# Pairing products and outputs on TensorE, and the chain's residue before the last corner's sum

## Chip, cores and metric

The kernel runs on one core of a Trainium2 chip. The metric is the device time of one execution in microseconds; the time before is the median of three runs.

## What is computed

x is 2 x 1024 x 256 in float32. A first layer adds a product with one 256 x 256 matrix per batch element, chosen by a category id. The second layer is a mixture of one chosen MLP and two shared ones, with a gate made from the first token:

```python
x = x + einsum('bsd,bdh->bsh', x, W[cat_ids]) + b[cat_ids][:, None, :]
s0, s1 = relu(x @ swi[0]) @ swo[0], relu(x @ swi[1]) @ swo[1]
eo = relu(x @ wi[type]) @ wo[type]                      # D=256, F=1024
w = softmax(relu(concat(eo[:, 0], s0[:, 0], s1[:, 0]) @ g1) @ g2)
x = x + eo * w[:, 0] + s0 * w[:, 1] + s1 * w[:, 2]
```

## The kernel before

Every float32 matrix is split into a rounded part (hi) and a residue (lo), both fp32r, and every product is a triple of matmuls: hi by hi, hi by lo, lo by hi (`three`, line 750). A tile is 128 partitions by 512 tokens.

The MLPs run as six passes over pairs of 512-token tiles, four groups of 256 hidden features each: groups j = 0 to 23. Groups 0 and 1 are computed directly. Groups 2 to 23 use seven products instead of eight for the 2 x 2 block product (hidden features by input features by two token tiles). TensorE runs product 1, then adds products 6, 7 and 4 into the same PSUM bank, `chain`; after each of the first three ScalarE copies the bank's running value into `kept` (line 396). Product 2 goes to the bank `left`, product 5 to `right`, product 3 is added to `right`. VectorE (line 534) adds kept 0 to left, makes `corner` = right + kept 2 between products 5 and 3, and adds kept 1 to right after product 3. The four hidden tiles are thus left (i = 0), chain (1), corner (2), right (3). For each ScalarE writes h_hi = relu (line 408) and VectorE the residue h_lo (line 529), in the order 0, 2, 1, 3. Product 1 of the next group may start once h_lo of chain is made, product 5 once h_lo of right is made, product 3 once corner is made, and products 6, 7 and 4 once kept 0, 1 and 2 are copied.

The outputs of group j, u = 0 to 7, are triples too: hidden tile u // 2 times one of two weight blocks, added up over four groups in the banks acc. They are run inside group j + 1, among its products, in an order written out by hand. In short, p for products of group j and o for outputs of group j - 1: p1 p2 o0 p6 p5 o1 p7 o2 o3 p4 p3 o4 o5 o6 o7.

Each engine runs its instructions in program order. Special groups carry more work behind or between the hidden tiles:

- Group 2: ScalarE casts three parts of x (line 389), VectorE makes their residues (line 516). Group 3: ScalarE casts four tiles of input sums (line 415), one before h_hi of corner, one between h_hi of corner and of chain, two at the end. Groups 5, 6, 9, 10: two such casts at the end.
- Groups 4, 8, 12, 16: ScalarE copies acc of a finished pass into y (line 487) behind h_hi of right; output 0 and 1 of the next group wait for it. Groups 5, 9, 13, 17: VectorE does the same for the other side (line 693), then gate partial sums (lines 550, 553).
- Group 18: VectorE reduces the gate (line 567) behind h_lo of right, ScalarE gathers the result with four copies (line 502), VectorE goes on. Group 19: softmax (lines 596 to 604, exponentials on ScalarE, line 506) and additions of whole tiles to x (line 612). Group 20: additions from acc (line 623), one behind h_lo of corner and one behind h_lo of chain, then more tiles.

GpSimd makes the sums of weight blocks (lines 290, 304), the weight residues m_lo and the residues of the input sums; weights come by DMA two groups ahead.

Of the kernel before, what the change touches and what calls it, by code (L numbers as in the profile page):

```python
# [46 lines left out]
def build(nc, x_t, cat_w, cat_b, mlp_w, ids, g1, g2, out_t):  # L47
# [7 lines left out]
    with ExitStack() as ctx:  # L55
# [150 lines left out]
        def nth(j, i):  # L206
            return i + 1 if j < DIRECT else NTH[i]
# [10 lines left out]
        def before(j, each):  # L218
            return (j - DIRECT) * each
# [294 lines left out]
        def _(dve):  # L514
# [12 lines left out]
            def hidden_lo(j, i):  # L527
                dve.wait_ge(h_hi_ready, 4 * j + nth(j, i))
                nc.vector.scalar_tensor_tensor(out=h_lo[:, j % 2, i, :], in0=hidden[i][:], scalar=0.0,  # L529
                                               in1=h_hi[:, j % 2, i, :].bitcast(F32), op0=ALU.max, op1=ALU.subtract  # L530
                                               ).then_inc(h_split, 1)
# [83 lines left out]
            def add_acc(q, side, d):  # L615
                kind, pair = PASSES[q]
                b, t = PAIRS[pair][side]
                dve.wait_ge(outputs_done, acc_done(q, side, d))
                if kind == 1:
                    dve.wait_ge(added[b][t], 1)  # L620
                else:
                    dve.wait_ge(added[b][t], 2 + d)
                nc.vector.scalar_tensor_tensor(out=x1_part(b, t, d), in0=acc[side][d][:], scalar=mix[:, b, kind:kind + 1],
                                               in1=x1_part(b, t, d), op0=ALU.mult, op1=ALU.add
                                               ).then_inc(last_added if kind == 2 else added[b][t], 1)
# [56 lines left out]
            for j in range(DIRECT, N):  # L682
                q = (j - 1) // GROUPS - 1
                dve.wait_ge(left_done, before(j, 1) + 1)
                dve.wait_ge(kept_ready, before(j, 3) + 1)
                add_kept(left, left, 0)
                if j == KEPT * GROUPS + 3:
                    gate_spread()
                if j % GROUPS == 1 and q >= 0:
                    for d in range(DC):  # L690
                        if q < KEPT:
                            dve.wait_ge(outputs_done, acc_done(q, 1, d))
                            nc.vector.tensor_copy(y_part(q, 1, d), acc[1][d][:]).then_inc(y_second, 1)
                        else:
                            add_acc(q, 1, d)
                hidden_lo(j, 0)
                if j == KEPT * GROUPS + 2:
                    gate_transpose()
                dve.wait_ge(right_done, before(j, 2) + 1)
                dve.wait_ge(kept_ready, before(j, 3) + 3)  # L700
                add_kept(corner, right, 2)
                hidden_lo(j, 2)
                if j == KEPT * GROUPS + GROUPS:
                    add_acc(KEPT, 0, 0)
                dve.wait_ge(right_done, before(j, 2) + 2)
                add_kept(right, right, 1)
                hidden_lo(j, 1)
                if j == KEPT * GROUPS + GROUPS:
                    add_acc(KEPT, 0, 1)
                hidden_lo(j, 3)  # L710
                if j == 2:
                    for n in range(3, 6):
                        part_lo_of(n)
                if j % GROUPS == 1 and 0 <= q < KEPT:
                    gate_partial(q)
                if j == KEPT * GROUPS + 2:
                    gate_quarters()
                    gate_logits()
                if j == KEPT * GROUPS + 3:
                    gate_max()  # L720
                    gate_softmax()
                    add_tile(0, 1)
                    add_tile(1, 0)
                if j == KEPT * GROUPS + 4:
                    add_tile(0, 0)
                    add_tile(1, 1)
                if j == KEPT * GROUPS + 5:
                    add_tile(2, 0)
                    add_tile(2, 1)
                if j == KEPT * GROUPS + 6:  # L730
                    add_tile(3, 0)
                    add_tile(3, 1)
# [13 lines left out]
        def _(pe):  # L746
# [116 lines left out]
            def product(j, n):  # L863
                q = j // GROUPS
                pair = PASSES[q][1]
                alpha, beta = PAIRS[pair]
                new_pair = j % GROUPS == 0 or j == DIRECT
                slot = j % SLOTS
                if n == 1:
                    pe.wait_ge(m_split, first_part(j))  # L870

                    pe.wait_ge(h_split, 4 * (j - 1) + nth(j - 1, 1))
                    if new_pair:
                        pe.wait_ge(part_split, 1 + max(part_no(alpha, 0), part_no(alpha, 1), part_no(beta, 1)))
                    three(chain, m_hi, A11, slot, *part(part_no(alpha, 0)), True, True).then_inc(chain_done, 1)
                if n == 2:
                    three(left, m_hi, A12, slot, *part(part_no(alpha, 1)), True, True).then_inc(left_done, 1)
                if n == 6:
                    if new_pair:
                        pe.wait_ge(t_split, 4 * pair + 2)  # L880
                    pe.wait_ge(m_split, second_part(j))
                    pe.wait_ge(kept_ready, before(j, 3) + 1)
                    three(chain, m_hi, S2, slot, *t_sum(pair, 1), False, True).then_inc(chain_done, 1)
                if n == 5:

                    pe.wait_ge(h_split, 4 * (j - 1) + nth(j - 1, 3))
                    three(right, m_hi, S1, slot, *t_sum(pair, 0), True, True).then_inc(right_done, 1)
                if n == 7:
                    if new_pair:
                        pe.wait_ge(t_split, 4 * pair + 3)  # L890
                    pe.wait_ge(kept_ready, before(j, 3) + 2)
                    three(chain, m_hi, S3, slot, *t_sum(pair, 2), False, True).then_inc(chain_done, 1)
                if n == 4:
                    if new_pair:
                        pe.wait_ge(t_split, 4 * pair + 4)
                    pe.wait_ge(kept_ready, before(j, 3) + 3)
                    three(chain, m_hi, A22, slot, *t_sum(pair, 3), False, True).then_inc(chain_done, 1)
                if n == 3:

                    pe.wait_ge(hidden_ready, before(j, 3) + 2)  # L900
                    three(right, m_hi, S4, slot, *part(part_no(beta, 1)), False, True).then_inc(right_done, 1)

            def output(j, u):
                i, d = u // DC, u % DC
                side, f = i // 2, (0, 1, 1, 0)[i]
                q = j // GROUPS
                first, final = j % GROUPS == 0 and i in (0, 2), j % GROUPS == GROUPS - 1 and i in (1, 3)
                if d == 0:
                    pe.wait_ge(h_split, 4 * j + nth(j, i))
                if u == 0 and j < DIRECT:  # L910
                    pe.wait_ge(m_split, second_part(j))
                if first:

                    if q == 0:
                        pe.wait_ge(x1_ready, 4 + side * DC + d + 1)
                    elif q <= KEPT:
                        pe.wait_ge((y_first, y_second)[side], (q - 1) * DC + d + 1)
                    else:
                        b, t = PAIRS[PASSES[q][1]][side]
                        pe.wait_ge(added[b][t], 2 + d)  # L920
                last = three(acc[side][d], m_hi, WO + f * D + d * P, j % SLOTS,
                             h_hi[:, j % 2, i, :], h_lo[:, j % 2, i, :], first, final)
                last.then_inc(outputs_done, 1)
# [20 lines left out]
            for u in range(8):  # L944
                output(0, u)
            for j in range(DIRECT, N):
                product(j, 1)
                product(j, 2)
                output(j - 1, 0)
                product(j, 6)  # L950
                product(j, 5)
                output(j - 1, 1)
                product(j, 7)
                output(j - 1, 2)
                output(j - 1, 3)
                product(j, 4)
                product(j, 3)
                for u in range(4, 8):
                    output(j - 1, u)
            for u in range(4):  # L960
                output(N - 1, u)
            for d, columns in ((0, slice(0, TOK)), (1, slice(0, TOK // 2)), (1, slice(TOK // 2, TOK))):
# [45 lines left out]
```

## Time and profile before

| | us |
|---|---|
| median of 3 runs | 268.51 (268.29 to 270.18) |
| the profiled execution | 268.48 |
| its span on the core | 266.6 |
| TensorE busy | 262.1 |
| VectorE, ScalarE, GpSimd busy | 163.4, 149.9, 162.2 |

Start times in the trace count from the span's start. A matmul's duration is modelled and overlaps the next one, so TensorE's pace is read from the distance of its starts. An engine's instruction may likewise start before the recorded end of the one ahead.

### The profile page before, as it was taken

The page shows a single profiled execution, that of the slowest core. Times are in us where ns is not written, and L with a number is a line of the kernel's source. Part 1 is how long each engine was busy: PE and PEld are TensorE (multiplying, and loading weights), DVE is VectorE, ACT ScalarE, POOL GpSimd, SP SyncE. Part 2 cuts the span into 40 slices and gives each one's busy share as a digit, 9 for nine tenths or more (in the row PEclk, how much of TensorE's full clock was granted, in tenths as well). Part 3 has the DMA queues.
Part 4 walks back from the last instruction along what each step waited for, and adds up shares of the span by engine and source line. Part 5 has one row for each costly group of instructions (what it writes and reads, how often), then busy time and mean ns, then how long its engine had stood idle before and what let it go on. Part 6 is the DMA issues. An engine that isn't in the chain of part 4 may idle for free.

```text
span 266.6 us, 3455 instructions
## 1 busy us (share of the span) xinstructions
PE 262.1 (98%) x1158; PEld 217.1 (81%) x1158; DVE 163.4 (61%) x246; ACT 149.9 (56%) x267; POOL 162.2 (61%) x171
## 2 busy tenths in 40 slices
PE   7999999999999999999999999999999999999995
PEld 7788888888888888888888888888888888888884
DVE  3779968635645435654445565345476577985664
ACT  3596457766576555665655744646545755645320
POOL 0269999999958949838944725625626528535000
DMA  5744322012022012102022012022022022000404
GB/s 167 216 168 157 121 79 80 14 69 80 1 81 79 18 61 79 68 16 79 0 79 81 26 53 81 9 71 80 2 79 79 0 79 76 6 0 0 157 4 157
DMA packets 7473, 18.31 MB, mean 69 GB/s; under 512 B 1312, under 2 KB 2080, under 8 KB 7456
## 3 DMA queue, kind: packets, MB, share of 16 engines
q1 hardware_dynamic: 6736, 16.92, 19.2%
q10 hardware_dynamic: 720, 1.18, 1.4%
q8 instruction: 9, 0.15, 0.2%
q14 instruction: 8, 0.07, 0.1%
HBM read 16.00 MB, written 2.10 MB: 68 GB/s over the span
## 4 chain that ended last, share of the span: by engine, by line
PE 97%; DMA 1%; DVE 1%; issue 0%; DVEq 0%
PE acc L750 48%; PE chain L750 23%; PE right L750 12%; PE left L750 6%; PE acc L759 4%; DMA x<-x_t 1%; PE left L805 1%; PE chain L805 1%; PE corner L750 1%; PE corner L805 1%; PE right L805 1%; DVE x_hi L640 0%; DVE x_lo L516 0%; DVE x L741 0%; DVEq L740 0%
## 5 line engine op out<-in xcount | busy, mean ns | idle before, releaser
L290 POOL TENSOR_TENSOR m_lo<-staged,m_hi 128x512 fp32r<-128x512 f32 (+2 forms) x49 | 82.9, 1704 | 76.5 <-ACT m_hi L372 62.5
L750 PE MATMUL acc<-h_lo,m_hi 128*128 128x512 f32 x190 | 73.9, 389 | 0.0
L750 PE MATMUL acc<-h_hi,m_lo 128*128 128x512 f32 x190 | 73.9, 389 | 0.0
L750 PE MATMUL acc<-h_hi,m_hi 128*128 128x512 f32 x190 | 73.9, 389 | 0.0
L396 ACT COPY kept<-chain 128x512 f32<-128x512 f32 x66 | 38.8, 587 | 52.7 <-PE chain L750 52.7
L750 PEld LDWEIGHTS acc<-h_hi,m_hi 128*128 128x128 f32 x190 | 35.7, 188 | 7.5
L750 PEld LDWEIGHTS acc<-h_lo,m_hi 128*128 128x128 f32 x190 | 35.7, 188 | 7.4
L750 PEld LDWEIGHTS acc<-h_hi,m_lo 128*128 128x128 f32 x190 | 35.7, 188 | 7.4
L529 DVE SCALAR_TENSOR_TENSOR h_lo<-left,h_hi 128x512 fp32r<-128x512 f32 x24 | 16.6, 691 | 28.2 <-ACT h_hi L408 28.2
L290 POOL TENSOR_TENSOR staged<-staged 128x128 f32<-128x128 f32 x66 | 31.0, 485 | 1.7
L534 DVE TENSOR_TENSOR left<-left,kept 128x512 f32<-128x512 f32 x22 | 15.3, 695 | 23.3 <-PE left L750 23.3
L529 DVE SCALAR_TENSOR_TENSOR h_lo<-corner,h_hi 128x512 fp32r<-128x512 f32 x24 | 16.6, 690 | 16.3 <-ACT h_hi L408 16.3
L534 DVE TENSOR_TENSOR corner<-right,kept 128x512 f32<-128x512 f32 x22 | 15.4, 698 | 18.2 <-ACT kept L396 18.2
L750 PE MATMUL chain<-t_hi,m_lo 128*128 128x512 f32 x66 | 25.7, 389 | 0.0
L750 PE MATMUL chain<-t_hi,m_hi 128*128 128x512 f32 x66 | 25.7, 389 | 0.0
L750 PE MATMUL chain<-t_lo,m_hi 128*128 128x512 f32 x66 | 25.7, 389 | 0.0
L408 ACT ACTIVATE h_hi<-right 128x512 fp32r<-128x512 f32 x24 | 14.4, 599 | 18.7 <-DVE right L534 18.3
L408 ACT ACTIVATE h_hi<-corner 128x512 fp32r<-128x512 f32 x24 | 14.4, 601 | 18.4 <-DVE corner L534 18.3
L372 ACT CAST m_hi<-staged 128x896 fp32r<-128x896 f32 x22 | 20.8, 944 | 0.0
L529 DVE SCALAR_TENSOR_TENSOR h_lo<-right,h_hi 128x512 fp32r<-128x512 f32 x24 | 16.6, 690 | 3.1 <-ACT h_hi L408 0.3
L290 POOL TENSOR_TENSOR t_lo<-t_raw,t_hi 128x512 fp32r<-128x512 f32 x12 | 15.3, 1294 | 2.5 <-ACT t_hi L415 2.5
L529 DVE SCALAR_TENSOR_TENSOR h_lo<-chain,h_hi 128x512 fp32r<-128x512 f32 x24 | 16.3, 680 | 0.3 <-ACT h_hi L408 0.3
(151 smaller groups left out, 439.8 us busy)
## 6 DMA issues: line engine op xcount, KB each, us to landing
staged<-mlp_w SPq DMA_DIRECT2D x22, 512.0 KB, 3.3
x<-x_t ACTq DMA_DIRECT2D x4, 256.0 KB, 3.6
staged<-mlp_w SPq DMA_DIRECT2D x4, 256.0 KB, 3.2
x<-x_t SPq DMA_DIRECT2D x4, 256.0 KB, 5.0
out_t<-x SPq DMA_DIRECT2D x2, 512.0 KB, 4.8
g_sb<-g SPq DMA_DIRECT2D x1, 768.0 KB, 3.8
out_t<-x SPq DMA_DIRECT2D x3, 256.0 KB, 2.3
w_raw<-cat_w SPq DMA_DIRECT2D x4, 128.0 KB, 2.4
```

Source lines behind the costliest of these rows:

```text
L290: return nc.gpsimd.tensor_tensor(out, a, b, ALU.subtract)
L372: nc.scalar.copy(m_hi[:, j % SLOTS, 0:PLAIN], staged[:, j % 2, 0:PLAIN]).then_inc(m_hi_ready, 1)
L396: nc.scalar.copy(kept[:, n, :], chain[:]).then_inc(kept_ready, 1)
L408: nc.scalar.activation(h_hi[:, j % 2, i, :], hidden[i][:], ACT.Relu).then_inc(h_hi_ready, 1)
L529: nc.vector.scalar_tensor_tensor(out=h_lo[:, j % 2, i, :], in0=hidden[i][:], scalar=0.0, in1=h_hi[:, j % 2, i, :].bitcast(F32), op0=ALU.ma ...
L534: nc.vector.tensor_tensor(out[:], product[:], kept[:, n, :], ALU.add).then_inc(hidden_ready, 1)
L750: last = nc.tensor.matmul(out[:, columns], half[:, slot, at:at + P], moving[:, columns], start=(start and n == 0), stop=(stop and n == 2), ...
L759: return nc.tensor.matmul(acc[t][d][:], w[:, b, at:at + P], x_part(x, b, t, i), start=start, stop=stop)
L805: return nc.tensor.matmul(hidden[i][:], w[:, 0, at:at + P], moving, start=start, stop=stop, skip_group_check=True)
```

## The change

On TensorE the order inside a group becomes p1 p2 o0 o1 p6 p5 o2 o3 p7 o4 o5 p4 p3 o6 o7: two products, two outputs, throughout, with product 7 alone. On VectorE the residue of the chain's tile, `hidden_lo(j, 1)`, stands ahead of the sum into right instead of behind it. The instructions themselves, their tiles and their semaphores are the same.

```diff
@@ -702,9 +702,9 @@
                 hidden_lo(j, 2)
                 if j == KEPT * GROUPS + GROUPS:
                     add_acc(KEPT, 0, 0)
+                hidden_lo(j, 1)
                 dve.wait_ge(right_done, before(j, 2) + 2)
                 add_kept(right, right, 1)
-                hidden_lo(j, 1)
                 if j == KEPT * GROUPS + GROUPS:
                     add_acc(KEPT, 0, 1)
                 hidden_lo(j, 3)
@@ -944,19 +944,22 @@
             for u in range(8):
                 output(0, u)
             for j in range(DIRECT, N):
+
                 product(j, 1)
                 product(j, 2)
                 output(j - 1, 0)
+                output(j - 1, 1)
                 product(j, 6)
                 product(j, 5)
-                output(j - 1, 1)
-                product(j, 7)
                 output(j - 1, 2)
                 output(j - 1, 3)
+                product(j, 7)
+                output(j - 1, 4)
+                output(j - 1, 5)
                 product(j, 4)
                 product(j, 3)
-                for u in range(4, 8):
-                    output(j - 1, u)
+                output(j - 1, 6)
+                output(j - 1, 7)
```

## Rows read from the trace of the kernel before

**Rows 1.** The page: busy us (share of the span) and instructions of each engine.
```profile
PE 262.1 (98%) x1158; PEld 217.1 (81%) x1158; DVE 163.4 (61%) x246; ACT 149.9 (56%) x267; POOL 162.2 (61%) x171
```

**Rows 2.** The page: the chain that ended last, shares by engine.
```profile
PE 97%; DMA 1%; DVE 1%; issue 0%; DVEq 0%
```

**Rows 3.** Stretches: length, busy us of five engines, clock, DMA share, GB/s; group 6.
```profile
74.50:84.70 10.20, 10.20 (x47) 8.45 (x46) 5.16 (x8) 6.43 (x11) 6.63 (x5) 1.00 0.19 65
```

**Rows 4.** Timeline of TensorE: start us, duration, what; product 1 of groups 10, 11.
```profile
115.16 0.39 PE L750 MATMUL chain<-part_hi,m_hi 128*128 128x512 f32 x1
...
125.36 0.39 PE L750 MATMUL chain<-part_hi,m_hi 128*128 128x512 f32 x1
```

**Rows 5.** Timeline of ScalarE in group 10, from the third kept copy on.
```profile
120.12 0.59 ACT L396 COPY kept<-chain 128x512 f32<-128x512 f32 x1 [0.45 <-PE chain L750]
121.60 0.60 ACT L408 ACTIVATE h_hi<-corner 128x512 fp32r<-128x512 f32 x1 [0.90 <-DVE corner L534]
122.22 0.60 ACT L408 ACTIVATE h_hi<-chain 128x512 fp32r<-128x512 f32 x1
123.63 0.60 ACT L408 ACTIVATE h_hi<-right 128x512 fp32r<-128x512 f32 x1 [0.81 <-DVE right L534]
124.12 1.13 ACT L415 CAST t_hi<-t_raw 128x512 fp32r<-128x512 f32 x2
```

**Rows 6.** Timeline of VectorE in group 10, from the sum into corner on.
```profile
120.81 0.70 DVE L534 TENSOR_TENSOR corner<-right,kept 128x512 f32<-128x512 f32 x1 [0.92 <-ACT kept L396]
122.23 0.69 DVE L529 SCALAR_TENSOR_TENSOR h_lo<-corner,h_hi 128x512 fp32r<-128x512 f32 x1 [0.72 <-ACT h_hi L408]
122.84 0.69 DVE L534 TENSOR_TENSOR right<-right,kept 128x512 f32<-128x512 f32 x1
123.45 0.68 DVE L529 SCALAR_TENSOR_TENSOR h_lo<-chain,h_hi 128x512 fp32r<-128x512 f32 x1
124.26 0.69 DVE L529 SCALAR_TENSOR_TENSOR h_lo<-right,h_hi 128x512 fp32r<-128x512 f32 x1
```

**Rows 7.** Timeline around product 3 of group 4, whose release comes late.
```profile
59.77 0.70 DVE L534 TENSOR_TENSOR corner<-right,kept 128x512 f32<-128x512 f32 x1 [1.14 <-ACT kept L396]
...
60.52 0.19 PEld L750 LDWEIGHTS right<-part_hi,m_hi 128*128 128x128 f32 x1
...
60.71 0.40 PE L750 MATMUL right<-part_hi,m_hi 128*128 128x512 f32 x1
```

**Rows 8.** Timeline of ScalarE in group 8: the two copies into y.
```profile
103.73 1.07 ACT L487 COPY y<-acc 128x512 f32<-128x512 f32 x2
```

**Rows 9.** Timelines of ScalarE and VectorE, end of group 2 to left sum of 3.
```profile
42.45 1.65 ACT L389 CAST part_hi<-x 128x512 fp32r<-128x512 f32 x3
...
43.20 3.88 DVE L516 TENSOR_TENSOR part_lo<-x,part_hi 128x512 fp32r<-128x512 f32 x3
47.00 0.69 DVE L534 TENSOR_TENSOR left<-left,kept 128x512 f32<-128x512 f32 x1
```

**Rows 10.** Timelines of VectorE and ScalarE: gate reduction, gather, first kept copy of group 19.
```profile
206.47 0.68 DVE L567 TENSOR_REDUCE gate_quarter<-gate_blocks 128x16 f32<-128x512 f32 x1
...
207.18 0.88 ACT L502 COPY gate_all<-gate_quarter 32x16 f32<-32x16 f32 x4 [1.35 <-DVE gate_quarter L567]
207.97 0.57 ACT L396 COPY kept<-chain 128x512 f32<-128x512 f32 x1
```

**Rows 11.** Timelines of ScalarE and VectorE, end of group 19 and group 20.
```profile
217.34 0.19 ACT L506 ACTIVATION_READ_ACCUMULATOR exps<-logits,neg_max 128x1 f32 x1
...
220.55 0.69 DVE L534 TENSOR_TENSOR left<-left,kept 128x512 f32<-128x512 f32 x1
...
222.34 0.59 ACT L396 COPY kept<-chain 128x512 f32<-128x512 f32 x1
...
225.06 0.74 DVE L623 SCALAR_TENSOR_TENSOR x<-acc,mix,x 128x512 f32<-128x512 f32 x1
```

**Rows 12.** Timeline of ScalarE in group 9: idle time put down to issue.
```profile
112.30 0.60 ACT L408 ACTIVATE h_hi<-chain 128x512 fp32r<-128x512 f32 x1 [0.30 <-issue]
```

## The prediction

> **What bounds the kernel now.** I read the page first. TensorE is busy for 262.1 of 266.6 us [rows 1], and the chain that ended last is TensorE for 97% [rows 2]. The stretches of one group each show it exactly: 10.20 us of TensorE in 10.20 us, at clock 1.00, while VectorE, ScalarE and GpSimd stand at 5 to 6.6 us [rows 3]. So I looked at TensorE's starts: group 10 begins at 115.16 and group 11 at 125.36 [rows 4], 10.20 us for 15 triples of matmuls, T = 0.68 us each (0.2267 per matmul). Group j begins at S(j) = 115.16 + 10.20 x (j - 10). Nothing is idle between groups 2 and 23, so a new order of the same 45 matmuls has nothing to win there; it can only lose, where a triple must now wait for ScalarE or VectorE. The question is how late their results come against the new slots.
>
> **The timetable of an ordinary group.** The order before is p1 p2 o0 p6 p5 o1 p7 o2 o3 p4 p3 o4 o5 o6 o7, after it is p1 p2 o0 o1 p6 p5 o2 o3 p7 o4 o5 p4 p3 o6 o7 (p a product of group j, o an output of group j - 1). p7 moves from slot 6 to 8, p4 from 9 to 11, p3 from 10 to 12, p6 from 3 to 4. From the group's start, before [rows 5, 6]: the third kept copy 4.96, the sum into corner 5.65, h_hi of corner 6.44, its h_lo 7.07, h_hi of chain 7.06, sum into right 7.68, h_lo of chain 8.29, h_hi of right 8.47, its h_lo 9.10. After: p7 ends at 9T = 6.12 instead of 4.76, 1.36 later, and so are the copy (6.32), the sum (7.01), h_hi of corner (7.80) and its h_lo (8.43). p4 ends at 12T = 8.16; h_hi of chain came 0.26 behind p4's end (7.06 against 6.80), so it is at 8.42 and ends 0.60 later. h_lo of chain then starts at 9.05 and lasts 0.68, to 9.73. The sum into right is now behind it: VectorE's next instruction started 0.61 after the one before (122.23, 122.84, 123.45), so it starts at 9.66; h_hi of right follows 0.79 later at 10.45, its h_lo at 11.08. **All that stands behind h_hi of right comes 1.98 us later against the groups' starts**, that is 1.36 from the slots and 0.62 from the new place of the residue.
>
> **When a late result costs.** The one place of before where a result comes at the last moment: the sum into corner ends at 59.77 + 0.70 = 60.47, the weights are loaded at 60.52, the matmul starts at 60.71, on its slot (within 0.01) [rows 7]. So a result that ends 0.19 us or more before the slot costs nothing; later, the excess is lost for good, since TensorE has no idle time to give back. In the ordinary group p1 of the next group (slot 10.20) may not overwrite chain before that h_lo ends at 9.73: wanted 10.01, margin 0.28. p3 wants the corner sum at 8.16 - 0.19 = 7.97 and has it at 7.71. p4 wants the third copy (end 6.91) at 7.29. p6 has gained a slot. So 0 there.
>
> The Trainium skill's page VectorE: DVE Perf Modes (The DRAIN you can't avoid) says that the next operation does not start until the pipe is empty, and adds that one not held starts earlier. The rows bear out only the second, 0.61 from start to start beside 0.69 to 0.70 of duration [rows 6]; by the first the residue would end 0.08 later, margin 0.20, and the sum would grow by some 0.3 in all.
>
> **The groups with extra work**, each against its slot less 0.19:
> - Group 2. Behind h_hi of right ScalarE casts three parts (1.65 for three, 0.53 apart [rows 9]). Before that cost nothing. After they start at 10.94, the first kept copy of group 3 at 12.52 and ends (0.59) at 13.10; its reader p6 has slot 10.20 + 4T = 12.92, wanted 12.73: **0.36**. VectorE's part residues and what follows took 3.80 from their start to the left sum (43.20 to 47.00 [rows 9]); they start at S(2) + 11.69 = 45.17, the left sum of group 3 at 48.97. The third copy stands 1.79 behind the left sum on ScalarE where ScalarE sets the pace (220.55, 222.34 [rows 11]): 50.76, ends 51.35; the corner sum 51.45 to 52.15. Slot of p3: 43.69 + 0.36 + 8.16 = 52.21, wanted 52.02: **0.14**. Behind it come h_hi of corner (52.24), the cast of t_hi(1,1) that the code puts there (0.50 each), and only then h_hi of chain at 53.25, h_lo from 53.88 to 54.56. p1 of group 4 wants 54.20: **0.37**. Its p6, behind two more casts, loses about **0.09**.
> - Groups 4, 8, 12, 16. ScalarE copies two accumulators into y, 1.07 for both, 0.48 apart [rows 8]. They now start at 10.94, the first ends at 11.53. It frees acc for the next group's o0, slot 11.56, wanted 11.37: **0.15** each, four times, **0.60**. Before, the first copy was done 1.8 us ahead of that slot. The term is the least certain, since the row gives only the two copies' common length: between 0 (if the first ends by 11.37) and 0.3 each. The second copy and o1 have 0.2 in hand.
> - Groups 5, 6, 9, 10 cast two tiles (1.13 [rows 5]); the kept copy then ends at 12.54, wanted 12.73: nothing, margin 0.19.
> - Gate reductions, group 18. gate_quarter stands behind h_lo of right at 206.47, the four gather copies on ScalarE start 0.71 later, and the kept copy of group 19 is queued 0.79 behind them [rows 10]. After: 11.69, 12.40, 13.19, ends 13.77, wanted 12.73: **1.04** at p6 of group 19.
> - Softmax, group 19. ScalarE's last accumulator read starts at 217.34 and takes 0.19 [rows 11], 1.47 behind the start of h_lo of right (206.96 + 9.10). After it ends at 12.54; the kept copy ends at 13.13: **0.40** at p6 of group 20. VectorE's softmax and tile additions hold the left sum until 220.55, 4.49 behind the same start: after, 5.37 into group 20, or 4.97 with the 0.40 counted; third copy 6.76 to 7.35, corner sum to 8.15, wanted 7.97 to 8.02: **0.17** over p4 and p3. Here the code also puts an accumulator's addition (0.74 long, so 0.66 to the next start by the overlap of 0.08 seen above [rows 11]) between corner's residue and chain's; h_lo of chain starts at 10.14 and ends 10.82, wanted 10.18: **0.63** at p1 of group 21. In groups 21 and 22 the left sum starts about 4.3 and 3.9 into the next group, and the third copy is due 1.79 later at the earliest, before its normal 6.32: nothing.
> - The tail: h_lo of right of group 23 ends at 11.77, its outputs have slots from 20T = 13.60; the last additions wait for TensorE as before: nothing. GpSimd's residues of t move up to 2.4 us, and are needed at slots that moved too: nothing.
>
> **Sum:** 0.36 + 0.14 + 0.37 + 0.09 = 0.96; + 0.60 = 1.56; + 1.04 = 2.60; + 0.40 + 0.17 + 0.63 = 3.80. The profiled execution took 268.48 (span 266.6), the median is 268.51: **272.3 us**, slower by 1.4%.
>
> **Rivals.**
> 1. Ordinary groups stall as well. For it: the margin is 0.28, and once ScalarE starts h_hi of chain with 0.30 of "issue" ahead of it [rows 12]. Both that and 0.08 more on VectorE in each group would miss by 0.10, in some 16 groups 1.6, and the starts of groups 4 and 21 would pay 0.38 more each: 273.9 to 274.7. Against: one such gap in 22 groups. 18%.
> 2. The lateness is 1.36, not 1.98, because the sum into right is not really held behind the residue. Then p6 of 19 loses 0.42, groups 8, 12, 16 nothing, group 3's p6 and group 20's p6 nothing; with the residues' 0.37 and 0.63 left: 269.9, say 270.0, within 1%. Against: both become ready within 0.01 us and the queue is in order. 12%.
> 3. The other side, not slower: TensorE makes up what it loses. If after a stall matmuls came closer than 0.2267 us, say by 0.011, the 3.80 us would be back after some 350 of 990 matmuls and the time would be 268.5. It decides once any spacing falls below 0.22. Against: 0.2267 holds through every stretch, behind the late release at 60.71 too, where the next ones came at 0.23. 6%. The Trainium skill (TensorE: Matmul & The Clock Gate, Back-to-back issue gap) gives 512/2.4 + 2.5, about 216 ns, which would be this rival; no stretch here shows it.
> 4. It becomes faster: TensorE would need idle time to lose, and has none. 2%.
>
> My forecast keeps 62%. **The range** is 270.0 (rival 2) to 275.5 (rival 1 at 274.7, with 0.8 more for the bounds of the twelve special places). About 1% is what a measurement can tell from no change: faster by more 2%, within 1% 19% (rivals 2, 3 and a low edge of the forecast), slower by more 79%.
>
> **What would show it.** TensorE's groups 6 to 18 still 10.20 apart, but for 0.15 at o0 of 9, 13, 17; group 19 about 11.2 long, group 20 about 11.4; h_hi of right 10.45 behind a group's start; waits of TensorE's weight loads on ScalarE's kept copy (19, 20), on the y copies, and on h_lo of chain (4, 21). Wrong would be a group of 10.20 at 19 (no queueing behind the gather copies), or every group longer than 10.25 (margin misjudged).

## The result

| | before | after |
|---|---|---|
| median of the executions, us | 268.4 (268.14 to 270.18) | 278.06 (277.73 to 278.14) |
| profiled execution, its span | 268.48, 266.6 | 278.13, 276.2 |

Each side has four executions here. The ratio is 1.0345, 95% interval 1.0316 to 1.0374: slower by 9.7 us, where 3.8 were forecast and the range ended at 275.5. The direction and the places first named held, the size did not.

The page of the changed kernel (busy us and share; then the chain that ended last, shares by engine) against [rows 1, 2]:

```profile
PE 267.1 (97%) x1158; PEld 216.0 (78%) x1158; DVE 169.7 (61%) x246; ACT 148.5 (54%) x267; POOL 161.7 (59%) x171
...
PE 77%; DVE 10%; ACT 5%; issue 3%; DMA 3%; ACTq 0%; DVEq 0%
```

The instructions are the same and as many. TensorE was the chain for 97%; now VectorE and ScalarE hold it for 15%. VectorE is busy 6.3 us longer with the same 246 instructions: something slowed some of them, and nothing in the prediction said so. The stretches of single groups (columns as in [rows 3]), groups 11, 14, 18, 19, 20, 22 of the changed kernel, show where:

```profile
127.01:137.21 10.20, 10.20 (x47) 8.45 (x45) 4.70 (x8) 6.34 (x11) 8.70 (x11) 1.00 0.01 3
157.81:168.56 10.75, 10.64 (x47) 8.22 (x45) 7.88 (x12) 5.30 (x9) 5.15 (x6) 1.00 0.11 29
199.40:210.27 10.87, 10.76 (x46) 8.21 (x45) 8.38 (x13) 5.29 (x9) 5.15 (x6) 1.00 0.12 36
210.27:221.78 11.51, 10.50 (x46) 8.38 (x46) 6.63 (x16) 6.87 (x17) 5.10 (x6) 1.00 0.17 57
221.78:235.78 14.00, 12.17 (x46) 9.20 (x45) 10.65 (x16) 6.08 (x14) 5.49 (x6) 0.89 0.12 39
246.24:257.38 11.14, 10.62 (x46) 8.20 (x45) 8.60 (x10) 5.29 (x9) 3.64 (x2) 1.00 0.01 1
```

Read as lengths: an ordinary group is still 10.20, as forecast. Group 19 loses 1.31 (forecast 1.04). Groups 14, 18 and 22 lose 0.55, 0.67 and 0.94 where nothing was forecast, group 20 loses 3.80 instead of 1.20 and is, with the first matmul of group 21, the only stretch below clock 1.00. (Losses are against the same group before, 10.20 here.)

The cause stands on VectorE's and GpSimd's timelines. Group 20 after (start us, duration, what), first VectorE's additions of two tiles, then GpSimd's weight residues:

```profile
224.74 4.34 DVE L612 SCALAR_TENSOR_TENSOR x<-y,mix,x 128x1024 f32<-128x1024 f32 x2
229.00 0.69 DVE L534 TENSOR_TENSOR left<-left,kept 128x512 f32<-128x512 f32 x1
...
225.50 2.50 POOL L290 TENSOR_TENSOR m_lo<-staged,m_hi 128x896 fp32r<-128x896 f32 x1 [5.22 <-ACT m_hi L372]
```

and the same in the kernel before:

```profile
218.15 2.48 DVE L612 SCALAR_TENSOR_TENSOR x<-y,mix,x 128x1024 f32<-128x1024 f32 x2
...
219.54 4.33 POOL L290 TENSOR_TENSOR m_lo<-staged,m_hi 128x896 fp32r<-128x896 f32 x2 [4.78 <-ACT m_hi L372]
```

Before, the additions start 1.39 us ahead of GpSimd's residues and take 2.48; it is GpSimd that is long, 4.33 for two where 3.38 to 3.50 is its usual. One addition is some 1.2 us from start to start of the next, so GpSimd arrived while the second of the two was running. After, GpSimd starts only 0.76 behind VectorE, during the first addition, gets in between the two, and the second waits: 4.34, which is 1.86 more. (In the kernel before, group 21 has the same picture as group 20, with GpSimd at 4.15.)

Groups 14 and 18 have the gate sums in this place. Group 18 before, VectorE then GpSimd:

```profile
196.27 2.25 DVE L553 SCALAR_TENSOR_TENSOR gate_part<-g_sb,y,gate_part 128x256 f32<-128x256 f32 x4
...
199.14 3.50 POOL L290 TENSOR_TENSOR m_lo<-staged,m_hi 128x896 fp32r<-128x896 f32 x2 [4.90 <-ACT m_hi L372]
```

and after:

```profile
200.88 3.92 DVE L553 SCALAR_TENSOR_TENSOR gate_part<-g_sb,y,gate_part 128x256 f32<-128x256 f32 x4
...
201.79 2.15 POOL L290 TENSOR_TENSOR m_lo<-staged,m_hi 128x896 fp32r<-128x896 f32 x1 [4.22 <-ACT m_hi L372]
```

Before, the sums were over at 198.52, 0.62 ahead of GpSimd; after, GpSimd starts 0.91 behind their first. GpSimd's place in the group is the same, 2.38 from its start; VectorE's moved. Group 14 is alike (2.25 before, 3.93 after). Of VectorE's instructions those that read two operands from SBUF grow longer, and no others. All gate sums of the changed kernel (count, shortest/median/longest ns) show one such wait per collision, 2158 ns where 484 is usual; before, the longest of the ten was 485:

```profile
L553 DVE SCALAR_TENSOR_TENSOR gate_part<-g_sb,y,gate_part x10: 476/484/2158, 77.6 to 204.3; 128x256 f32<-128x256 f32 x10
```

The sums that take one operand from PSUM (line 534) and the residues h_lo keep their 0.69.

The way from there to TensorE is one of queues. ScalarE in group 20 after:

```profile
225.69 0.59 ACT L396 COPY kept<-chain 128x512 f32<-128x512 f32 x1 [0.28 <-PE chain L750]
229.78 0.60 ACT L408 ACTIVATE h_hi<-left 128x512 fp32r<-128x512 f32 x1 [3.50 <-PE acc L750]
...
230.78 0.59 ACT L396 COPY kept<-chain 128x512 f32<-128x512 f32 x1
```

The left sum ends at 229.69 on VectorE; h_hi of left waits for it at the head of ScalarE's queue (the row names a TensorE output, which had long been done), and the third kept copy, which could have started at about 228.4 (0.20 behind the end of product 7, as in group 10 before), stands behind and starts at 230.78. Product 4 starts 1.93 us late.

### The profile page after: what moved, and what is told of

The parts are those of the page before. It is cut to its first block, busy times and chain, and to the rows that moved or that the text cites. A ratio compares the mean times of both kernels' runs of the same rounds, so it can differ in the third digit from the quotient of the medians.

```text
span 276.2 us, 3455 instructions
## 1 busy us (share of the span) xinstructions
PE 267.1 (97%) x1158; PEld 216.0 (78%) x1158; DVE 169.7 (61%) x246; ACT 148.5 (54%) x267; POOL 161.7 (59%) x171
## 3 DMA queue, kind: packets, MB, share of 16 engines
q10 hardware_dynamic: 720, 1.18, 1.3%
## 4 chain that ended last, share of the span: by engine, by line
PE 77%; DVE 10%; ACT 5%; issue 3%; DMA 3%; ACTq 0%; DVEq 0%
PE acc L750 38%; PE chain L750 19%; PE right L750 10%; PE left L750 5%; DVE h_lo L529 3%; PE acc L759 3%; DMA x<-x_t 3%; DVE gate_part L553 2%; ACT h_hi L408 2%; ACT kept L396 2%; DVE corner L534 1%; DVE x L612 1%; DVE right L534 1%; DVE left L534 1%; ACT m_hi L376 1%
## 5 line engine op out<-in xcount | busy, mean ns | idle before, releaser
L750 PE MATMUL acc<-h_hi,m_hi 128*128 128x512 f32 x190 | 74.8, 394 | 0.1
L290 POOL TENSOR_TENSOR staged<-staged 128x128 f32<-128x128 f32 x66 | 31.7, 495 | 1.7
L750 PE MATMUL chain<-t_hi,m_hi 128*128 128x512 f32 x66 | 26.5, 401 | 3.7 <-ACT kept L396 3.3
L408 ACT ACTIVATE h_hi<-left 128x512 fp32r<-128x512 f32 x24 | 14.4, 602 | 10.7 <-DVE left L534 7.2
L750 PEld LDWEIGHTS chain<-t_hi,m_hi 128*128 128x128 f32 x66 | 12.4, 187 | 9.3 <-issue 5.0
```

The lines of the kernel that those rows point to most:

```text
L290: return nc.gpsimd.tensor_tensor(out, a, b, ALU.subtract)
L408: nc.scalar.activation(h_hi[:, j % 2, i, :], hidden[i][:], ACT.Relu).then_inc(h_hi_ready, 1)
L750: last = nc.tensor.matmul(out[:, columns], half[:, slot, at:at + P], moving[:, columns], start=(start and n == 0), stop=(stop and n == 2), ...
```

## The experiments

**GpSimd steps aside.** In the changed kernel, GpSimd waits with its first weight residue until VectorE is through (the weights of group j are split during group j - 1, so j == 15 acts in group 14):

```diff
                 # in split_group(j), ahead of the first m_lo
+                if j == 15:
+                    pool.wait_ge(gate_sums, 8)
+                if j == 19:
+                    pool.wait_ge(gate_sums, 12)
+                if j == 21:
+                    pool.wait_ge(added[1][1], 1)
+                if j == 22:
+                    pool.wait_ge(added[1][0], 1)
+                if j == 23:
+                    pool.wait_ge(added[1][0], 2)
```

> The changed kernel, with GpSimd's first weight residue held back until VectorE's gate sums (groups 14, 18) and whole-tile additions (groups 20, 21, 22) are done. Theory A, both engines working from SBUF at once slows VectorE: the four gate sums take 2.2 us again instead of 3.9, the two tile additions 2.5 instead of 4.3, groups 14, 18, 22 lose under 0.2 us, group 20 about 1.3 instead of 3.8, TensorE's clock stays at 1.00: 273.2 us. Rival B, VectorE was slow for a reason of its own (landing DMAs, its operands): durations stay, about 278 or above.

272.85 us, ratio 1.0151 (1.0097 to 1.0206). The tile additions take 2.48 for two again and the gate sums 2.25 for four. Stretches of groups 14, 18, 19, 20, 22:

```profile
157.40:167.60 10.20, 10.20 (x47) 8.45 (x45) 6.45 (x12) 5.50 (x9) 5.12 (x6) 1.00 0.16 53
198.39:208.59 10.20, 10.20 (x46) 8.45 (x45) 7.07 (x13) 5.50 (x9) 5.12 (x6) 1.00 0.14 51
208.59:219.89 11.30, 10.48 (x46) 8.37 (x45) 6.40 (x16) 6.87 (x17) 5.11 (x6) 1.00 0.14 46
219.89:231.25 11.36, 10.85 (x46) 8.06 (x45) 8.00 (x15) 5.85 (x13) 5.11 (x6) 1.00 0.13 37
241.56:251.76 10.20, 10.20 (x47) 8.45 (x45) 7.00 (x10) 5.50 (x9) 3.37 (x2) 1.00 0.00 0
```

So the collision is shown to be worth 5.2 us of the 9.7. With it gone, the two largest places of the forecast's timetable are close: group 20 was forecast at 11.40 and is 11.36, group 19 at 11.24 and is 11.30. The whole, forecast at 272.3, is 272.85. That the sum is so close (the groups lose 4.1 us together, forecast 3.8) is partly luck, since smaller terms were off in both directions: groups 3 and 4 lose 0.63 where 0.96 was forecast, the y copies 0.94 where 0.60 was, and group 10 loses 0.15 where nothing was.

The Trainium skill states this (SBUF — State Buffer, Who interferes with whom): VectorE with two SBUF inputs contends with a GpSimd instruction that reads SBUF, and "Issue order, not op shape, decides who blocks". The traces of the two kernels agree with both halves: 4.33 on GpSimd before, 4.34 on VectorE after.

**The same in group 20 alone** (only the wait of j == 21).

> The changed kernel, with GpSimd held back in group 20 alone. Theory A: only that group changes, 14.0 us to about 11.5, no matmul at 0.427 us spacing, since TensorE's 1.9 us of idle time ahead of product 4 is gone; groups 14, 18 and 22 lose what they lose in the changed kernel: 275.3 us. Rival: the clock falls in this stretch whatever the idle time is, then at least 1.6 us stays: 277.

276.15 us, 1.0268 (1.0214 to 1.0323); 275.3 was expected. Group 20 is 11.37, groups 14, 18 and 22 lose 0.55, 0.66 and 0.98 as before. But group 21 is 11.72: there GpSimd and VectorE collide (additions 4.33), and output 4, which waits for VectorE's additions from acc, starts 1.32 late. The expectation took 2.6 us off the profiled execution of the changed kernel, which had its half clock in group 20 and no waiting VectorE in group 21. At full clock that kernel's group 20 is 13.23 and its group 21 collides as well (last experiment), so 1.86 is what the wait saves; 278.06 less 1.86 is 276.2.

**TensorE's order alone**: the diff's second hunk without the first.

> Only TensorE's new order; VectorE keeps the sum into right ahead of the chain's residue. By the timetable the residue ends 0.6 us later than in the changed kernel, 10.33 after the group's start where 10.01 is wanted: every group loses 0.3 to 0.4 us, group length 10.5 to 10.6, in all 276 to 280 us. Rival, both orders of VectorE are alike because product 3 ends too late for the sum: group length 10.20 and about 274.

279.5 us, 1.038 (1.0313 to 1.0447). VectorE and then TensorE at the end of group 9:

```profile
118.38 0.70 DVE L534 TENSOR_TENSOR right<-right,kept 128x512 f32<-128x512 f32 x1
118.98 0.68 DVE L529 SCALAR_TENSOR_TENSOR h_lo<-chain,h_hi 128x512 fp32r<-128x512 f32 x1
```

```profile
119.31 0.39 PE L750 MATMUL acc<-h_hi,m_lo 128*128 128x512 f32 x1
119.81 0.47 PE L750 MATMUL chain<-part_hi,m_hi 128*128 128x512 f32 x1
120.12 0.40 PE L750 MATMUL chain<-part_lo,m_hi 128*128 128x512 f32 x1
```

The residue ends at 119.66, product 1 starts at 119.81, 0.27 behind its slot (119.31 + 0.23), and its second matmul comes at 0.31 instead of 0.23. The groups are 10.47 to 10.61 long, but for group 20, which is 12.98. The wanted margin of 0.19 was right to 0.05, and the moved residue is what makes the new order bearable in ordinary groups. Without it, groups 14, 18 and 19 lose nothing beyond that: the gate sums take 2.25 for four and are clear of GpSimd. That each group's own loss gives VectorE and ScalarE this time back is a reading and was not tested. Group 20 has the collision here too (additions 4.34): product 4 comes 1.34 late and product 1 of group 21 waits 1.18. So not all of the 10.5 us of this version are the residue's place.

**The residue's swap alone**: the first hunk without the second.

> Only VectorE's swap; TensorE keeps its old order. All behind h_hi of right is 0.6 us later instead of 2.0: ordinary groups 10.20, the first kept copy of group 19 0.3 late, group 20 a few tenths: 268.7 to 269.5 us. Rival, the swap is the source of most of the loss (queueing on VectorE): above 271.

273.27 us, 1.0149 (1.0088 to 1.021), far above the 269.5 expected. All ordinary groups are 10.20 and group 19 is 10.60; group 20 holds nearly all the rest (groups 19 and 20; groups 4 and 5 lose 0.2 together):

```profile
208.75:219.35 10.60, 10.46 (x46) 8.37 (x45) 6.39 (x16) 6.89 (x17) 5.08 (x6) 1.00 0.16 49
219.35:233.59 14.24, 12.12 (x46) 9.46 (x45) 11.53 (x17) 5.87 (x13) 5.46 (x6) 0.88 0.12 38
```

VectorE's additions start at 220.96, 0.6 us later against the group than before, GpSimd's residue at 221.74; that is enough for GpSimd to get in between, and the additions take 4.35. The collision has an edge, not a slope: product 4 comes 2.27 late with 0.6 us of lateness, and 1.93 late with the changed kernel's 2.0. The expectation counted lateness and left the edge out. About 1.6 us of group 20's 14.24 are matmuls at half clock; three of the four executions had such a stretch (granted clock 0.993 or 0.994, 272.76 to 274.72 us), the one at clock 1.000 took 272.01. So here, unlike in the changed kernel, the half clock may have part in the median.

**ScalarE's copies into y in its idle time**, on top of the first experiment:

```diff
                 hidden_hi(j, 1)
-                hidden_hi(j, 3)
                 q = j // GROUPS - 1
                 if j % GROUPS == 0 and 0 <= q < KEPT:
                     ...
+                hidden_hi(j, 3)
```

> The changed kernel with GpSimd held back, and ScalarE's two copies into y moved ahead of h_hi of right, into its idle time behind h_hi of chain. Timetable theory: the waits of output 0 in groups 5, 9, 13, 17 (0.82 us together in the kernel with GpSimd held back) are gone and nothing else: 0.8 us below that kernel, 1.012 of the kernel before. Rival, ScalarE is late for another reason (PSUM reads collide): no gain.

271.69 us, 1.0128 (1.0072 to 1.0185). In the profile groups 5, 13 and 17 are 10.20; group 9 is 10.20 too. The gain in the ratio is 0.6 us and within the intervals; the groups carry the reading: the four stalls, 0.94 us by the groups' lengths, are gone. Group 10 stays at 10.38.

**Gate copies and exponentials behind the first kept copy**, on top of the last (the two blocks of lines 502 and 506 moved behind `keep(j, 0)` of groups 19 and 20):

> As the last, and ScalarE's gather copies and exponentials queued behind the first kept copy of groups 19 and 20 instead of ahead of it. Timetable theory: group 19 goes from 11.3 to 10.2 us and group 20 loses 0.3 less: 1.3 us below the last, 1.007 of the kernel before. Rival, VectorE, which now gets the gathered gate later, passes the delay on to the left sum and the third kept copy: group 19 stays above 10.8.

270.86 us, 1.0078 (1.0055 to 1.01). Group 19 is 10.20. Group 20 stays 11.36: its wait moved from product 6 (0.23) to product 4 (0.06 before, 0.40 now), because VectorE's left sum is the later of the two anyway. So 1.1 gained by the groups' lengths and 0.8 by the medians, not 1.3: the rival held in group 20, not in 19.

**Casts, part residues and the addition of group 20 cleared away**, on top of the last: of the three casts of group 2 two ahead of the third kept copy and one ahead of h_hi of right, two of its residues into VectorE's gaps, t_hi(1,1) and t_hi(1,2) behind h_hi of chain, and `add_acc(KEPT, 0, 0)` ahead of h_lo of corner.

> As the last, and the casts and residues of groups 2 and 3 and VectorE's addition of group 20 moved out of the way of the first kept copy and of h_lo of chain. Timetable theory: groups 3, 4 and 21 start 0.4, 0.2 and 0.7 us earlier; what is left is below 0.5 us: 1.002 of the kernel before, the same within 1%. So TensorE's new order costs nothing by itself. Rival, the order itself costs something (bank switches, weights): ordinary groups longer than 10.20, 1.007 or more.

269.27 us, 1.0019 (0.9992 to 1.0046), no different from before. Its groups 4, 19 and 20:

```profile
54.00:64.20 10.20, 10.20 (x46) 8.45 (x45) 4.69 (x8) 6.90 (x12) 10.04 (x11) 1.00 0.12 40
207.16:217.36 10.20, 10.20 (x46) 8.45 (x45) 6.40 (x16) 6.98 (x17) 5.10 (x6) 1.00 0.15 51
217.36:228.15 10.79, 10.55 (x47) 8.22 (x46) 8.09 (x15) 5.96 (x13) 5.10 (x6) 1.00 0.09 24
```

TensorE's new order costs nothing by itself in an ordinary group, and brings nothing: about 9.2 of the 9.7 us were work of the other engines placed for the old order. What is left, 0.5 us by the medians, cannot be told from nothing there, but the trace shows where it lies: group 20 is 10.79 (product 4 waits 0.39 for the third kept copy, behind the left sum) and group 10 is 10.36. No version beat the kernel before, which had no idle time left to win.

**The half clock.** In the profiled execution TensorE ran some eight matmuls of group 20 at a spacing of 0.427 instead of 0.227 us, right behind its idle time ahead of product 4 (granted clock 0.50 in the stretch 234 to 236, the 1.2 GHz level). The kernel with the swap alone did so too. (Each run below is one execution.) To see whether idle time alone brings it, tiny copies on ScalarE were put ahead of the third kept copy of group 10 in the kernel before:

```diff
+                if j == 10:
+                    act.wait_ge(chain_done, before(j, 4) + 3)
+                    for i in range(n):
+                        nc.scalar.copy(fill[:, 4 * i:4 * i + 4], ones[:, 0:4])
                 keep(j, 2)
```

> The kernel before, with twelve tiny copies on ScalarE ahead of the third kept copy of group 10, so that TensorE idles some 2.2 us ahead of product 4 in an otherwise ordinary group. Theory C, idle time of about 2 us alone makes the clock fall: matmul spacing 0.43 us for some eight matmuls behind it, granted clock under 1, 1.6 us lost on top of the idle time. Rival, it needs what group 20 has besides (VectorE's burst, landing DMAs): spacing stays 0.227 and only the idle time is lost.

With n = 12 (8 columns each) product 4 came 0.66 late, not 2.2: the copies follow each other at 0.10 us, where 0.22 had been taken. The clock did not fall, and an idle time this short answers nothing.

> The kernel before with 20 tiny copies (0.10 us each) on ScalarE ahead of the third kept copy of group 10; with 12 the matmul of product 4 came 0.66 us late, so about 1.45 us late here, like product 6 of group 19 in the changed kernel (1.18). Theory C: clock 1.00, only the idle time is lost. Rival: the clock falls here too.

> 27 copies: product 4 some 2.15 us late, between the two places where the clock fell (1.93 and 2.27). Theory C, the idle time alone makes it fall: spacing 0.43 us for some eight matmuls behind, 1.6 us lost on top. Rival, it needs what group 20 has besides: spacing stays 0.227.

> 34 copies: product 4 some 2.85 us late. Theory C: the clock falls, for as long or longer than with 27 copies. Rival: it stays at 1.00.

Product 4 came 1.37, 2.04 and 2.70 us late, and TensorE's clock stayed at 1.00 in all three. Idle time of this length alone did not make it fall there. Two more: 27 copies in nine groups (6, 8, ... 22) of one execution, and in group 20 alone.

> The kernel before with 27 tiny copies on ScalarE ahead of the third kept copy of groups 6, 8, ... 22: nine idle times of TensorE of about 2 us in one execution. Theory D, the clock falls behind some such idle times and not others, by where they lie: one or more of the nine show spacing 0.43 us for some matmuls. Theory E, only what surrounds group 20 (VectorE's additions, landing output or weight DMAs) brings it: none falls outside group 20.

> The same with group 20 alone, 3 us before the place where the clock fell in the two kernels. Theory E: it falls here as it did there, 1.6 us on top of some 2.1 us. Theory D: either.

Groups 6 and 14 of the first:

```profile
74.97:89.07 14.10, 12.22 (x46) 9.42 (x45) 5.29 (x9) 8.96 (x39) 7.64 (x6) 0.88 0.15 49
171.97:184.48 12.51, 10.63 (x47) 8.29 (x45) 6.04 (x10) 7.85 (x36) 5.12 (x6) 1.00 0.14 43
```

Behind seven of nine idle times of 2.0 to 2.4 us the clock fell, for 1.5 to 1.6 us more; behind those of groups 14 and 22 it did not. With group 20 alone it fell. So group 20's own work is not needed, and an idle time of about 2 us brings the half clock at most places but not at all. Neither the length nor the place in the kernel decides: product 4 of group 10 came 2.04 late in two executions, and the clock fell in the one with nine idle times and not in the one with a single one; and in group 20 of the changed kernel it fell behind 1.93 us and, in the execution below, not behind 1.92. What decides stays open.

**Does it matter in the median?** Three of the four timed executions of the changed kernel had clock 1.000 and took as long as the profiled one.

> The changed kernel itself, once more. Three of its four timed executions had a granted clock of 1.000 and the same time as the profiled one with 0.994. If the half-clock stretch only covers losses that come without it, then at clock 1.00 group 20 is about 1.5 us shorter, and the start of group 21 and group 21 itself are as much longer (the residue's 0.6 us wait, a collision of VectorE's tile additions with GpSimd): 277 to 279 us in all. Rival, the stretch is a loss of its own: about 276.5 us at clock 1.00.

278.63 us, all at clock 1.00. Groups 20 and 21:

```profile
221.74:234.97 13.23, 10.96 (x47) 8.06 (x45) 9.87 (x15) 5.85 (x13) 5.50 (x6) 1.00 0.11 40
234.97:246.71 11.74, 10.61 (x45) 8.44 (x46) 10.94 (x13) 5.30 (x9) 5.53 (x6) 1.00 0.00 1
```

Together 24.97, against 24.46 (14.00 and 10.46) in the execution with half clock. At full clock TensorE reaches product 1 of group 21 earlier and waits 0.62 for the residue, as forecast, and VectorE's additions collide again in group 21 (4.34 for two; output 4 starts 1.29 late). In this kernel the half clock took the place of losses that come without it; it is no cause of the 9.7 us.

## Why the prediction was right or wrong

- **What bounds, and that nothing is to win: right.** Ordinary groups stayed at 10.20, and the cleared version cannot be told from the kernel before.
- **The timetable of the ordinary group: right.** h_hi of right starts 10.44 behind group 2's start (44.28 against 33.84), forecast 10.45. The wanted 0.19 held within 0.05 (residue left in its old place: 0.27 late where 0.32 follows from the rule).
- **The price of a late result: a small term too small.** A late product also delays its own second matmul by 0.07 to 0.11. For the y copies 0.15 was forecast; groups 9, 13 and 17 lost 0.20, which is 0.10 at output 0 and the rest mostly at its second matmul. Group 5 lost 0.35. The row that the 0.19 was read from, [rows 7], had a trace of this: in group 4 of before the matmuls behind that release slip by 0.05 together, and the group is 10.25 long. The term for the casts of group 9 was put at nothing with a margin of 0.19; group 10 lost 0.16, in steps of 0.05 and less at products 1 and 6.
- **Gate gather: 1.04 forecast, 1.31 measured** in the changed kernel, where group 18 itself ended late; 1.10 with GpSimd aside. Right.
- **Group 3 and the start of group 4: 0.87 forecast, 0.43 measured.** The 3.80 us taken from [rows 9] for the part residues held a collision with GpSimd of its own (GpSimd's sum beside them took 1.77 where 1.29 is usual); moved, they took 2.73 (three from 45.52), still more than three of the shortest, 0.67 each. The left sum came 1.15 earlier in the group than forecast, and product 3 of group 3 and product 1 of group 4 hardly waited. The same mechanism as below, with the other sign.
- **The step that failed** is the one that costs VectorE's extra work at the durations of before: "softmax and tile additions hold the left sum until ... 4.49 behind the same start", and, for groups 21 and 22, the words "before its normal 6.32: nothing"; the gate sums at the start of groups 14 and 18 have no term at all. The work slid by 1.98 us into GpSimd's 2.1 us weight residue, which no row shown ahead of the prediction had for these groups: GpSimd's timeline was not laid beside VectorE's new one. Each collision cost 1.7 to 1.9 us on VectorE, and reached TensorE through h_hi of left in ScalarE's queue. The rest of the chain was right: with GpSimd aside the left sum of group 20 starts 5.37 into the group, as forecast, and with 1.86 added it would start at 7.23 and the third kept copy at 9.02; in the changed kernel they start at 7.22 and 9.00. Between the changed kernel and the one with GpSimd aside, groups 14, 18, 20 and 22 differ by 0.55, 0.67, 2.64 and 0.94, groups 15, 19 and 21 by 0.4 together, 5.2 in all; at full clock, groups 20 and 21 differ by 1.87 and 1.43.
- **Rival 1** (ordinary groups stall too) did not happen, except that group 9's gap of [rows 12] came again and had a part in group 10's 0.16. **Rival 2** (1.36 instead of 1.98) fell: h_hi of right came at 10.44, and the swap alone delays it by 0.6 (group 10: 9.08 for 8.47). **Rival 3** (TensorE makes up) fell: between groups 2 and 23 ten spacings in a row took 2.26 us or more in every run. The range's upper end was built from margins of ordinary groups and of the terms named, and had nothing in it for a duration that changes with its place.

## What to carry to other kernels

When work moves in time, its durations move too, if it shares something with another engine: lay the new times of every VectorE instruction with two SBUF operands against GpSimd's timeline, and treat an overlap as a full wait of one for the other's instruction, whichever starts second; in a run of such instructions the waiting engine gets in between two of them. A row that is longer in one place than its like elsewhere (GpSimd's 4.33 for 3.4, the part residues' 3.88 for 2.73) can be the sign of such a collision in the trace of before, and the moved work may inherit it or lose it. An order tuned on the one engine that bounds the kernel also holds the queues of all others: a change of it that wins nothing there can only disturb them.

## What the runs showed of the hardware

- A GpSimd residue of 128x896 holds off a VectorE instruction with two SBUF operands for up to 1.7 us (484 to 2158 ns), and the additions of two tiles for 1.86. Which side waits depends on 0.6 us of timing: behind the start of two additions by 0.76 to 0.90 us, GpSimd got in between them (groups 20 and 22, changed kernel); by 1.39 to 1.61, it waited for both (groups 20 and 21 before, group 21 in the changed kernel's execution with half clock).
- A TensorE product released late delays its second matmul as well, by 0.07 to 0.11 us.
- Idle time of TensorE of 2.0 to 2.4 us was followed by eight or so matmuls at 1.2 GHz at eight of the ten places tried in the last two runs, and at none of three tries of 1.4 to 2.7 us in group 10 alone, though group 10 was among the seven where nine groups of one execution had it. In the changed kernel, 1.93 us brought it in one execution and 1.92 us did not in another. Idle times of 0.6 to 1.4 us never brought it in the traces kept.
